# Folding the eight masked expert blocks to 128 columns before the turn, and putting the mask back behind it, in a one-core attention and expert kernel

## The reference

```python
logits = einsum('th,eh->te', xf, gate_w)          # xf: layernorm(x), 256 x 512
onehot = one_hot(argmax(logits), 8)               # each token has one expert
g = einsum('th,ehd->etd', xf, wg)                 # 8 experts, 128 columns each
u = einsum('th,ehd->etd', xf, wu)
inter = square(relu(g)) * u * onehot.T[:, :, None]
out = einsum('etd,edh->th', inter, wd)            # 8 x 128 rows into 512 columns
x = x + out
```

## Time and profile before

| what | value |
|---|---|
| median of 3 runs | 576.09 us (575.88 to 576.16) |
| the profiled execution, its own time | 576.21 us |
| its span, first to last instruction | 574.4 us |
| TensorE matmul busy | 568.8 us, 99% of the span |
| VectorE busy | 456.3 us, 79% |
| ScalarE busy | 401.3 us, 70% |
| chain that ended last | TensorE 96%, ScalarE 2%, VectorE 1% |

### The profile page before, as it was taken

How to read it: one execution, slowest core, us unless ns; L and a number is a source line. 1 busy time by engine, 2 the same in 40 slices (tenths; PEclk the granted TensorE clock), 3 DMA queues, 4 the chain that set the end, 5 groups by cost and what they waited for, 6 DMA issues and landing times.

```text
span 574.4 us, 8076 instructions
## 1 busy us (share of the span) xinstructions
PE 568.8 (99%) x3010; PEld 477.8 (83%) x3010; DVE 456.3 (79%) x495; ACT 401.3 (70%) x543; POOL 1.7 (0%) x7
## 2 busy tenths in 40 slices
PE   9999999999999999999999999999999999999998
PEld 5888888888888888888888888888888887877887
DVE  5987878787878797889888988887878788887742
ACT  6776767676777787778777777776767785697321
POOL 1000000000000000000000000000000000000000
DMA  8668787768677877787877788776687652100201
GB/s 322 220 200 261 219 240 239 228 217 239 218 228 249 260 249 228 252 256 245 227 261 257 243 232 257 222 220 222 217 275 235 202 169 110 38 1 2 75 0 38
DMA packets 33239, 115.90 MB, mean 202 GB/s; under 512 B 4080, under 2 KB 4784, under 8 KB 32944
## 3 DMA queue, kind: packets, MB, share of 16 engines
q1 hardware_dynamic: 32768, 115.05, 63.2%
q10 hardware_dynamic: 432, 0.33, 0.2%
HBM read 114.84 MB, written 0.52 MB: 201 GB/s over the span
## 4 chain that ended last, share of the span: by engine, by line
PE 96%; ACT 2%; DVE 1%; issue 0%; POOL 0%; POOLq 0%
PE ps L967 95%; ACT w L550 1%; PE ps L1059 0%; PE ps L1229 0%; PE ps L1316 0%; DVE st L745 0%; DVE x_s L743 0%; DVE h_s L761 0%; DVE sm_s L832 0%; DVE aTs L855 0%; PE ps L1198 0%; ACT st L480 0%; ACT qk L385 0%; POOL wz L378 0%; DVE st L756 0%
## 5 line engine op out<-in xcount | busy, mean ns | idle before, releaser
L967 PE MATMUL ps<-nh,zh 128*128 128x512 f32 x388 | 142.7, 390 | 0.0
L967 PE MATMUL ps<-nl,zh 128*128 128x512 f32 x388 | 142.6, 389 | 0.0
L967 PE MATMUL ps<-nh,zl 128*128 128x512 f32 x388 | 142.5, 389 | 0.0
L654 DVE TENSOR_TENSOR zl<-zf,zh 128x1024 fp32r<-128x1024 f32 x49 | 60.1, 1226 | 80.2 <-ACT zh L385 80.2
L644 DVE TENSOR_TENSOR nl<-rawn,nh 128x1024 fp32r<-128x1024 f32 x96 | 113.9, 1219 | 0.9 <-issue 0.6
L633 DVE TENSOR_TENSOR tl<-rawt,th 128x1024 fp32r<-128x1024 f32 x96 | 113.0, 1216 | 1.1 <-ACT th L385 1.0
L385 ACT ACTIVATE nh<-rawn 128x1024 fp32r<-128x1024 f32 x96 | 99.8, 1057 | 10.6 <-DMA rawn<-in_ctxn 9.8
L385 ACT ACTIVATE th<-rawt 128x1024 fp32r<-128x1024 f32 x96 | 96.5, 1052 | 2.0 <-DMA rawt<-in_ctxt 2.0
L416 ACT ACTIVATE zf<-ps 128x512 f32<-128x512 f32 x98 | 58.2, 597 | 56.5 <-PE ps L967 51.0
L967 PEld LDWEIGHTS ps<-nl,zh 128*128 128x128 f32 x388 | 72.8, 188 | 15.2
L967 PEld LDWEIGHTS ps<-nh,zl 128*128 128x128 f32 x388 | 72.8, 188 | 15.1
(11 more groups left out here) (177 smaller groups left out, 614.6 us busy)
## 6 DMA issues: line engine op xcount, KB each, us to landing
rawn<-in_ctxn SPq DMA_DIRECT2D x97, 512.0 KB, 6.5
rawt<-in_ctxt SPq DMA_DIRECT2D x96, 512.0 KB, 4.9
h_s<-in_wg SPq DMA_DIRECT2D x4, 512.0 KB, 7.1
h_s<-in_wu SPq DMA_DIRECT2D x4, 512.0 KB, 6.9
wds<-in_wd SPq DMA_DIRECT2D x4, 512.0 KB, 4.3
raw<-in_ctxt SPq DMA_DIRECT2D x2, 512.0 KB, 8.6
h_s<-in_wvt SPq DMA_DIRECT2D x2, 512.0 KB, 6.9
wq_s<-in_wq SPq DMA_DIRECT2D x1, 1024.0 KB, 9.7
```

Of the source, the lines that this page charges most:

```text
L654: e.tensor_tensor(zl[b % 2][:], zf[:], zh[b % 2][:], ALU.subtract).then_inc(*s.zl.mark(b))
L967: return e.matmul(o, w, x, start=start, stop=stop)
```

## The change

A token has one expert, so of its eight blocks of 128 columns seven are zero. The changed kernel sums the eight blocks to one of 128 columns, turns that one, and multiplies it behind the turn by a mask that has been turned as well.

- `route` also writes the token's expert number 128 columns wide (`ixw`).
- `fold(r, 0)` sums blocks 0 to 3 of `it` (now 9 blocks in one tile) into block 8, and `fold(r, 1)` blocks 4 to 8 into `itc`; both read the tile with the columns outside and the blocks, 512 bytes apart, inside.
- TensorE turns `itc` with one matmul for a half, and `ixw` of both halves with one each, in the first half's group.
- `hot_turned(r)` compares the turned numbers with 0 to 7: a mask `hot` of 8 times 128 columns. ScalarE copies the turned block to `tih`, VectorE makes the rest `til`. `dealt(r, g)` multiplies two blocks of the mask by each of them, giving `ith` and `itl` for experts 2g and 2g + 1.
- `down` takes a list of experts and waits for each pair. The first half's second layer is one run of 24 matmuls, with the second half's turn in its middle. The second half does six experts 512 columns wide into bank 7 and the last two in two sides of 256. VectorE adds bank 7 to `x1` ahead of the sides.

```diff
@@ route @@
+                e.tensor_copy(ixw[r][:], ixf[:, r:r + 1].to_broadcast([P, P])).then_inc(*s.gt.mark(("wide", r)))
@@ VectorE: inter, turned @@
                 if r:
-                    e.wait_ge(*s.ti.of((r - 1, k)))
-                e.tensor_tensor(it[k][:], bank(UB[k][1]), g2[k][:], ALU.mult).then_inc(*s.it.mark((r, k)))
-
-            def turned(r, k):
-                e.wait_ge(*s.ith.of((r, k)))
-                e.tensor_tensor(itl[k][:], bank(IB[k]), ith[k][:], ALU.subtract).then_inc(*s.itl.mark((r, k)))
+                    e.wait_ge(*s.fold.of((r - 1, k)))
+                e.tensor_tensor(flat(it[:, 4 * k:4 * k + 4]), bank(UB[k][1]), g2[k][:], ALU.mult).then_inc(*s.it.mark((r, k)))
+
+            def fold(r, k):
+                e.wait_ge(*s.it.of((r, k)))
+                if k:
+                    e.wait_ge(*s.fold.of((r, 0)))
+                o, a = (itc[r][:], it[:, 4:9, :]) if k else (it[:, 8, :], it[:, 0:4, :])
+                e.tensor_reduce(o, a.rearrange("p e n -> p n e"), AX_X, ALU.add).then_inc(*s.fold.mark((r, k)))
+
+            def hot_turned(r):
+                e.wait_ge(*s.ti.of(0))
+                a = IC[r].rearrange("p (o n) -> p o n", o=1).to_broadcast([P, 8, P])
+                n = io_s[:].rearrange("p (e o) -> p e o", o=1).to_broadcast([P, 8, P])
+                e.tensor_tensor(hot[r][:], a, n, ALU.is_equal).then_inc(*s.om.mark(r))
+
+            def turned(r):
+                e.wait_ge(*s.tih.of(r))
+                e.tensor_tensor(til[r][:], bank(IB[r])[:, 0:P], tih[r][:], ALU.subtract).then_inc(*s.til.mark(r))
+
+            def dealt(r, g):
+                w = slice(2 * g, 2 * g + 2)
+                if g == 0:
+                    e.wait_ge(*s.om.of(r))
+                    e.wait_ge(*s.til.of(r))
+                for o, a, step in ((ith, tih, s.ith), (itl, til, s.itl)):
+                    a = a[r][:].rearrange("p (o n) -> p o n", o=1).to_broadcast([P, 2, P])
+                    e.tensor_tensor(o[r][:, w, :], hot[r][:, w, :], a, ALU.mult).then_inc(*step.mark((r, g)))
@@ VectorE: order @@
             inter(0, 0)
+            fold(0, 0)
             square(0, 1)
             inter(0, 1)
+            fold(0, 1)
             route(1, 1)
-            turned(0, 0)
             down_low(2)
             square(1, 0)
-            turned(0, 1)
             inter(1, 0)
+            hot_turned(0)
+            turned(0)
+            for g in range(4):
+                dealt(0, g)
             down_low(3)
-            e.wait_ge(*s.wd.of((0, 0)))
-            turned(1, 0)
+            hot_turned(1)
             square(1, 1)
+            fold(1, 0)
             inter(1, 1)
-            result(0, 0, (0, 1), bank(1), slice(0, D))
-            turned(1, 1)
+            fold(1, 1)
+            turned(1)
+            for g in range(4):
+                dealt(1, g)
+            result(0, 0, 0, bank(1), slice(0, D))
+            e.wait_ge(*s.wd.of((1, "wide")))
+            e.tensor_tensor(x1[:, 1, :], bank(7), x1[:, 1, :], ALU.add).then_inc(*s.x2.mark("x"))
+            e.wait_ge(*s.x2.of("x"))
@@ TensorE: order @@
-            e.wait_ge(*s.gt.of(("copy", 0)))
-            turn(0, 0)
             e.wait_ge(*s.gm.of((0, 0)))
             experts_up(1, 0, 0)
-            turn(0, 1)
+            e.wait_ge(*s.it.of((0, 0)))
             experts_up(1, 0, 1)
-            e.wait_ge(*s.gt.of(("copy", 1)))
-            down(0, 0, bank(1), slice(0, D), True).then_inc(*s.wd.mark((0, 0)))
-            e.wait_ge(*s.gm.of((0, 1)))
+            e.wait_ge(*s.fold.of((0, 1)))
+            e.wait_ge(*s.gt.of(("wide", 1)))
+            e.transpose(bank(IB[0])[:, 0:P], itc[0][:], id_s[:])
+            for r in range(2):
+                m = e.transpose(IC[r], ixw[r][:], id_s[:])
+            m.then_inc(*s.ti.mark(0))
             experts_up(1, 1, 0)
-            turn(1, 0)
             experts_up(1, 1, 1)
-            down(0, 1, bank(1), slice(0, D), True).then_inc(*s.wd.mark((0, 1)))
-            turn(1, 1)
+            down(0, bank(1), range(4), slice(0, D), True)
+            e.wait_ge(*s.fold.of((1, 1)))
+            e.transpose(bank(IB[1])[:, 0:P], itc[1][:], id_s[:]).then_inc(*s.ti.mark(1))
+            down(0, bank(1), range(4, 8), slice(0, D), True).then_inc(*s.wd.mark(0))
+            down(1, bank(7), range(6), slice(0, D)).then_inc(*s.wd.mark((1, "wide")))
             for i, (b, cols) in enumerate(SIDES):
-                if i == 1:
-                    e.wait_ge(*s.gm.of((1, 0)))
-                down(1, 0, bank(b)[:, 0:T], cols).then_inc(*s.wd.mark((1, 0, i)))
-            for i, (b, cols) in enumerate(SIDES):
-                down(1, 1, bank(b)[:, 0:T], cols).then_inc(*s.wd.mark((1, 1, i)))
+                down(1, bank(b)[:, 0:T], range(6, 8), cols).then_inc(*s.wd.mark((1, i)))
```

More of the change, by code:

```diff
@@ L119, in signals @@
     s.lneh, s.lnel, s.lg = (steps(n, range(2)) for n in ("lne_h", "lne_l", "lg"))
-    s.gt = steps("gt", [(n, r) for r in range(2) for n in ("copy", "max", "index", "float", "hot")])
+    s.gt = steps("gt", [(n, r) for r in range(2) for n in ("copy", "max", "index", "float", "hot", "wide")])
     rk = [(0, 0), (0, 1), (1, 0), (1, 1)]
     s.gu = steps("gu", [(r, k, j) for r, k in rk for j in range(2)])
-    s.gm, s.g2, s.it, s.ti, s.ith, s.itl = (steps(n, rk) for n in ("gm", "g2", "it", "ti", "ith", "itl"))
+    s.gm, s.g2, s.it, s.fold = (steps(n, rk) for n in ("gm", "g2", "it", "fold"))
+    s.ti, s.tih, s.til, s.om = (steps(n, range(2)) for n in ("ti", "tih", "til", "om"))
+    s.ith, s.itl = (steps(n, [(r, g) for r in range(2) for g in range(4)]) for n in ("ith", "itl"))
     s.wdh, s.wdl = (steps(n, range(4)) for n in ("wdh", "wdl"))
-    s.wd = steps("wd", [(0, 0), (0, 1), (1, 0, 0), (1, 0, 1), (1, 1, 0), (1, 1, 1)])
+    s.wd = steps("wd", [0, (1, "wide"), (1, 0), (1, 1)])
+    s.x2 = steps("x2", ["x"])
     s.o = steps("o", range(3))
@@ L170, in program @@
         w_s = several("w", 4, [P, 512])
+        hot = several("hot", 2, [P, 8, P])
         wvh = sb("wvh", [P, 4, D], F32R)
@@ L173, in program @@
         aTl, aTh = several("aTs", 2, [P, 4, T], F32R)
+        ith = several("ith", 2, [P, 8, P], F32R)
         wvl = sb("wvl", [P, 4, D], F32R)
@@ L250, in program @@
         g2 = [sb(f"g2{i}", [P, 512]) for i in range(2)]
-        it = [sb(f"it{i}", [P, 512]) for i in range(2)]
-        ith = [sb(f"ith{i}", [P, 512], F32R) for i in range(2)]
-        itl = [sb(f"itl{i}", [P, 512], F32R) for i in range(2)]
+        it = sb("it", [P, 9, P])
+        itc = [sb(f"itc{i}", [P, P]) for i in range(2)]
+        ixw = [sb(f"ixw{i}", [P, P]) for i in range(2)]
+        tih = [sb(f"tih{i}", [P, P], F32R) for i in range(2)]
+        til = [sb(f"til{i}", [P, P]) for i in range(2)]
+        itl = [sb(f"itl{i}", [P, 8, P], F32R) for i in range(2)]
         o_s = sb("o_s", [P, 2, D])
@@ L268, in program @@
         UB, IB = ((5, 7), (4, 0)), (3, 6)
+        IC = (bank(2)[:, 0:P], bank(2)[:, P:2 * P])
         SIDES = ((2, slice(0, T)), (5, slice(T, D)))
@@ L598, in square @@
                 e.activation(g2[k][:], gm[k][:], ACT.Square).then_inc(*s.g2.mark((r, k)))
-            def turned(r, k):
[L601 to L604, removed]
+            def turned(r):
+                e.wait_ge(*s.ti.of(r))
+                copy(tih[r][:], bank(IB[r])[:, 0:P]).then_inc(*s.tih.mark(r))
             norm_high(0, 6)
@@ L945, in _ @@
             inter(0, 0)
+            fold(0, 0)
             square(0, 1)
             inter(0, 1)
+            fold(0, 1)
             route(1, 1)
-            turned(0, 0)
             down_low(2)
             square(1, 0)
-            turned(0, 1)
             inter(1, 0)
+            hot_turned(0)
+            turned(0)
+            for g in range(4):
+                dealt(0, g)
             down_low(3)
-            e.wait_ge(*s.wd.of((0, 0)))
-            turned(1, 0)
+            hot_turned(1)
             square(1, 1)
+            fold(1, 0)
             inter(1, 1)
-            result(0, 0, (0, 1), bank(1), slice(0, D))
-            turned(1, 1)
+            fold(1, 1)
+            turned(1)
+            for g in range(4):
[4 more added lines that the diff above has]
+            e.wait_ge(*s.x2.of("x"))
             for i, (b, cols) in enumerate(SIDES):
-                result(1 + i, 1, (1, 1, i), bank(b)[:, 0:T], cols)
+                result(1 + i, 1, (1, i), bank(b)[:, 0:T], cols)
         @block.tensor
@@ L1311, in experts_up, with down @@
                 m.then_inc(*s.gu.mark((r, k, j)))
[L1313 to L1324, removed]
+            def down(r, o, experts, cols, wait_weights=False):
+                for x_ in experts:
+                    if cols.start == 0 and x_ % 2 == 0:
+                        e.wait_ge(*s.ith.of((r, x_ // 2)))
+                        e.wait_ge(*s.itl.of((r, x_ // 2)))
+                    if wait_weights and x_ % 2 == 0:
                         e.wait_ge(*s.wdl.of(x_ // 2))
-                    n = half(i)
```

(3 more changed lines are left out.)

## The result

Ten executions of each kernel, side by side: 578.31 us with the change (576.96 to 579.13), 576.12 before (575.70 to 576.90). The ratio is 1.0037, 95% interval 1.0029 to 1.0044: slower by 0.37%, 2.2 us. I had said 577.0, with a range from 576.2 to 578.0.

A forecast was written before the change was run, and what follows sets the result against it. TensorE, busy for 99% of the span, bounds the kernel: -1.38 us of its work plus a new 2.3 us wait for VectorE gives +0.9 us, so 577.0 us against a median of 576.09; range 576.2 to 578.0.

The forecast's parts named there:

- the line of VectorE and the wait: VectorE from inter(1, 0) to fold(1, 1) runs without a gap; TensorE waits 2.3 us before the second half's turn.
- as taken from `zsum`: Folds priced like zsum, the reduction whose inner step is not the next column: 1.08 and 1.31 us.
- the rate of columns in order: Folds at 0.69 and 0.82 us: a wait of 1.7 us before the turn, 576.5 us in all; chance 0.15.
- cheap folds: Rival: fold reductions run at the rate of columns in order, wait 1.7 us, time 576.5, or 576.2 with cheap deals; chance 0.15.
- a dearer line: Rival: VectorE's 17 instructions from inter(1, 0) to fold(1, 1) cost over 0.25 us more, time above 577.24; chance 0.26.
- the rival of the hidden wait: VectorE keeps ahead before the second half's turn, so TensorE gains its 1.38 us: 574.7 us; chance 0.03.
- the clock: Rival: TensorE's clock falls in the 2.3 us wait, slowing matmuls behind it: up to +7.1 us, 584; chance 0.05.
- Nothing in the trace shows it for a wait between matmuls, and I think this one too short: Reason given against TensorE's clock falling in the 2.3 us wait before the second half's turn; chance 0.05.
- a sign of being wrong: Matmuls behind the wait at the second half's turn 0.43 us apart would show the prediction wrong.
- which I cost at nothing: The two last output transfers, 128 KB each, leave 0.7 us apart instead of 1.4: no cost.
- Off the path, as said: Removed ScalarE copies, ixw in route(0), both halves' deals and bank 7's addition were said to cause no wait.
- The 1.38 us that the change takes off TensorE: Turns, extras behind them and matmuls removed, less those added, in the last layer: -1.38 us if nothing waits.

The follow-up runs named there:

- gap_long: The kernel before with eight additions on VectorE, results unused, that TensorE awaits in front of its last turn, a wait of 3.8 us: 581.99 us.
- before_gap: The kernel before with six additions on VectorE, results unused, that TensorE awaits in front of its last turn, a wait of 2.04 us: 578.38 us.
- fill8: The changed kernel with 8 matmuls of 512 columns, results unread, in front of the second half's turn: 577.27 us, ratio 1.0018.
- fill4: The changed kernel with 4 matmuls, results unread, in front of the second half's turn: 578.06 us.
- pad_best: best with the 22 idle matmuls at TensorE's start cut into 52 of 216 columns, padding its program to the old length: 574.95 us, ratio 0.9979.
- best: The changed kernel with down_low(3), hot_turned(1) taken from before fold(1, 1), the former to before inter(1, 0), the latter behind the fold; down_high(3) earlier: 575.39 us, ratio 0.9988.

## Why the prediction was wrong

**Right, almost to the hundredth: the line of VectorE and the wait.** Shifted by the 0.32 us by which this execution came to the layer earlier, the prediction had `inter(1, 0)` at 553.06 (measured 553.04), `square(1, 1)` at 560.10 (560.12), the turn at 563.8 (563.70), and TensorE there at 561.50 (561.48). The reductions were 1.07 and 1.23 to 1.31, as taken from `zsum`; the rate of columns in order would have made the wait 1.7. The rivals of cheap folds and of a dearer line both fell. (A slip without effect: the rival of the hidden wait counts 10.7 us of VectorE's line up to 561.8; there it is 8.4, and 10.7 only up to the turn at 564.1.) The two executions with neither of the two surprises below lie at 576.82 and 576.96; a third has the same span, 575.2, and 0.7 us more outside it.

**Wrong: the clock.** The step that failed is the sentence "Nothing in the trace shows it for a wait between matmuls, and I think this one too short", with a chance of 0.05. The fall came in nine of sixteen executions, going by a mean clock of 0.997; two of the nine are profiled and show it behind the wait, with the matmuls 0.43 apart that the prediction had named as a sign of being wrong. Its price was wrong too, in the other direction: I gave it +7.1, or 580 if the clock came back midway. It came back after 3.4 us, and about half of that is the 1.6 us it cost; the median of the nine is 578.35. The Trainium skill's rule that the array drops to the lower clock when the engine has been idle ("TensorE: Matmul & The Clock Gate", Part 1) agrees with this trace and with `gap_long`; `before_gap` shows that an idle stretch of 2.0 us need not do it. The likeliest case was therefore not one time but two, 576.9 and 578.4, and the second was the commoner.

**Wrong: the end.** The step "which I cost at nothing", of the output transfers. In four of the sixteen executions the clock stood at 1.000 and the span was still 576.6 to 577.3, at least 1.6 above the shortest, 575.0. In the profiles of fill8 and fill4 such an excess is a last transfer that lands 1.7 us late beside the code fetch; that the four have the same cause is likely, but none of them was profiled. It is not the distance between the two transfers that costs: pad_best has them just as close, and its executions lie together.

**Off the path, as said:** ScalarE's copies, `ixw`, the deals of both halves, the addition of bank 7.

The 1.38 us that the change takes off TensorE are real, and most of it shows as soon as VectorE has its line in another order: 574.95 us in `pad_best`, which also has the padding, 0.21% under the kernel before (interval 0.12% to 0.30%), with the change's arithmetic untouched; `best` without the padding measured 575.39.

## What to carry to other kernels

When a change takes work off the bounding engine by giving it to another, write out the second engine's line start by start, from the last point where the first engine feeds it: steps from rows gave the wait here to 0.1 us. Then price a new wait of the matmul engine at its length plus the chance of a half clock behind it, and look for instructions in the line that nobody needs yet; two of them, moved, were the whole wait. If neither goes, a few idle matmuls in the wait are cheap cover.

## What the runs showed of the hardware that was not expected

- A TensorE wait of 2.0 to 2.2 us let the granted clock fall to half in nine of sixteen executions of one kernel, in five of six of another, in two of seven of a third and in none of five of the kernel before with an added wait; one of 3.8 us in four of four; one of 0.3 us, after eight idle matmuls, in none of eleven. In the four profiles that have the fall it stayed down for 3.4 us, beginning 0.1 to 1.2 us behind the end of the wait.
- A fetch of 16 KB of code beside an output transfer went with 0.6 to 1.7 us more until landing, in eight profiles of eight.
- Summing in steps of 512 bytes costs 1.07 us for 512 columns instead of 0.68; storing in steps of 36 bytes costs 1.13 instead of 0.69. Turning the layout round only moved the cost.
